# Two FFNs beside a patch search on one core: a new order of work on all five engines, transposes by DMA, moments on the vector engine

## What is computed

```python
y = einsum('ncij,vc->nvij', patches, w_mask) / (x_norm * w_norm)
idx = argmax(y.reshape(NL, -1))                       # over 512 x 9
integrate = max_act * max_sim + w_mask[max_ch] * (1 - max_sim)
h = leaky_relu(concat([integrate, sim_map_max]) @ w_i1.T + b_i1, 0.2)
vcs = tanh(h @ w_i2.T + b_i2)
h2 = relu(vcs @ w_l1.T + b_l1) @ w_l2.T + b_l2        # then out_p = einsum with w_conv
x = x + fold(out_p)
def ffn(t): return qlinear(relu(qlinear(ln(t), W1, b1)), W2, b2)   # q: x, W, b to e5m2
t = t + ffn(t)                                        # FFN 0
xn = ln_c(x); s = (xn * xn).sum(axis=1)
x = x + xn / (2 + 1e-4 * conv5x5(s)) ** 0.75
t = t + ffn(t)                                        # FFN 1
```

## Time and profile before

| | us |
|---|---|
| median of 3 runs (lowest, highest) | 3559.91 (3558.04, 3561.16) |
| the profiled execution | 3554.84 |
| its span | 3553.0 |
| busy: PE, ACT, DVE, POOL | 3011.0, 2832.7, 2778.1, 2566.0 |
| PE's granted clock, mean | 0.958 |

### The profile page before, as it was taken

The page is one execution under the profiler, slowest core; times in us unless marked ns, Lnnn a source line. Parts: engine busy times, 40 slices in busy tenths (PEclk is TensorE's granted clock), DMA queues, the critical chain, the costliest instruction groups (busy, mean ns, idle before and its releaser), DMA issues. The chain is left out here.

```text
span 3553.0 us, 62660 instructions
## 1 busy us (share of the span) xinstructions
PE 3011.0 (85%) x18190; PEld 1688.2 (48%) x18190; DVE 2778.1 (78%) x10043; ACT 2832.7 (80%) x7303; POOL 2566.0 (72%) x3993
## 2 busy tenths in 40 slices
PE   5888888888888888888888888888888888888755
PEld 2444454454545445445544545454444555445432
DVE  6777888888888888888888888888888888888631
ACT  0444788888888888888888888888878888888977
POOL 2455787777778777777877777787777778777753
PEclk9999999999999999999999999999999999999855
DMA  3111121211112121111212111121212112121000
GB/s 88 38 45 47 45 63 52 65 54 57 61 57 62 52 67 51 57 61 56 62 52 67 52 58 60 57 62 52 66 51 64 55 57 62 52 66 42 24 31 35
DMA packets 64607, 195.78 MB, mean 55 GB/s; under 512 B 11394, under 2 KB 14732, under 8 KB 64268
## 3 DMA queue, kind: packets, MB, share of 16 engines
q1 hardware_dynamic: 54028, 172.89, 15.1%
q0 software_dynamic: 10240, 18.89, 2.1%
HBM read 134.72 MB, written 57.02 MB: 54 GB/s over the span
## 5 line engine op out<-in xcount | busy, mean ns | idle before, releaser
L527 ACT ACTIVATE ffn_hid<-banks 128x384 f16<-128x384 f32 x2304 | 1026.8, 487 | 260.0 <-PE banks L370 236.7
L393 PE MATMUL banks<-wcT,xc 128*128 128x512 f32 x2304 | 1187.8, 618 | 50.2 <-DVE mx L745 43.4
L745 DVE TENSOR_REDUCE mx<-banks 128x1 f32<-128x512 f32 x1152 | 781.4, 687 | 428.8 <-PE banks L393 427.6
L370 PE MATMUL banks<-ffn_xT,w1q 128*128 128x384 bf16 x2304 | 668.8, 343 | 177.3 <-ACT ffn_hid L527 138.0
L994 POOL TENSOR_TENSOR ffn_f<-ffn_y,b2q 128x864 f16<-128x864 f16 x256 | 465.3, 1818 | 288.3 <-DVE nb L731 209.7
L370 PEld LDWEIGHTS banks<-ffn_xT,w1q 128*128 128x128 bf16 x2304 | 226.1, 98 | 775.8 <-ACT ffn_hid L527 589.4
L393 PEld LDWEIGHTS banks<-wcT,xc 128*128 128x128 f32 x2304 | 414.5, 196 | 282.8 <-issue 140.8
L825 DVE TENSOR_SCALAR ffn_hid<-ffn_hid,b1q 128x1152 f16<-128x1152 f16 x768 | 405.8, 551 | 139.0 <-ACT ffn_hid L527 138.6
L996 POOL TENSOR_TENSOR x<-x,ffn_f 128x864 f32<-128x864 f32 x256 | 466.6, 1823 | 20.1
L560 ACT ACTIVATE ffn_x<-x,cols 128x96 fp8e5<-128x96 f32 x1152 | 461.3, 456 | 0.0
L560 ACT ACTIVATE ffn_x<-x,nb,roots 128x96 fp8e5<-128x96 f32 x1152 | 425.1, 456 | 0.0
(11 more groups left out here) (153 smaller groups left out, 4178.6 us busy)
## 6 DMA issues: line engine op xcount, KB each, us to landing
xt<-x_tok_in SPq DMA_DIRECT2D x128, 432.0 KB, 3.2
xc<-x_chan_in SPq DMA_DIRECT2D x128, 432.0 KB, 3.6
out_tok<-x SPq DMA_DIRECT2D x128, 432.0 KB
win<-x_tok_in,xrow POOLq DMA_INDIRECT x128, 2.6
wrow<-vector_table,vidx POOLq DMA_INDIRECT x128, 2.9
shift<-shift_in SPq DMA_DIRECT2D x1, 960.0 KB
vector_table<-wtab SPq DMA_DIRECT2D x1, 384.0 KB, 2.9
w1raw<-w_in SPq DMA_DIRECT2D x1, 288.0 KB
```

The lines of the kernel that those rows point to most:

```text
L370: last = pe.matmul(bank[:, 0:GW], w1q[:, ffn.layer, c * P:(c + 1) * P], ffn.xT[:, g * GW:(g + 1) * GW], start=True, stop=True)
L393: last = pe.matmul(ps_score[score_bank(j)], xc[p][:, j, :], wcT[:, :], start=True, stop=True)
L527: return nc.scalar.activation(dst, src, ACT.Copy)
L745: nc.vector.tensor_reduce(mx[p][:, j:j + 1], ps_score[score_bank(j)], AX.X, ALU.max).then_inc(score_taken, 1)
```

## The change

The fp8 pixels of an FFN are written in pairs, turned by a DMA transpose that SP issues (`turn`), and read by PE in place of the three transposing units; the nine hidden units are cut 512, 512, 128 columns wide. The moments move from POOL to DVE, where they alternate with the pick; three sums of the pick become one product and one reduction. POOL's two adds of an output are taken apart (`ffn_bias`, `ffn_output`). And the order of each engine's step is new. The diff, cut:

```diff
+COLUMNS = [(0, 512), (512, 1024), (1024, J * P)]
-UNITS = G + HC * G + 2
+UNITS = HC * G + 2
...
+                self.x8 = sb(f"{name}_x8", [P, PAIRS, P, 2], F8)
+                self.xT = sb(f"{name}_xT", [P, PAIRS, P], F16)
...
+            def turn(ffn, tile):
+
+                sp.wait_ge(ffn.x8_ready, tile + 1)
+                wait_past(sp, ffn.filled, tile * UNITS - 2)
+                sp.dma_start_transpose(ffn.xT[:, :, :], ffn.x8[:].rearrange("p a c t -> p (a c t)").bitcast(F16)
+                                       ).then_inc(ffn.turned, 16)
...
+            def body(k):
+                if k.back is not None:
+                    turn(ffn0, k.back)
+                if k.pre is not None:
+                    turn(ffn1, k.pre)
+                load(Step(k.k + 1))
                 if k.rtail is not None:
                     sp.wait_ge(x4_ready, k.rtail + 1)
...
-                        for i in range(J // G):
-                            last = pe.matmul(bank[0:C, i * P:(i + 1) * P], ffn.x8[:, u * G + i, :],
-                                             ident_b[:, :], start=True, stop=True)
...
+                            pe.wait_ge(ffn.turned, (tile + 1) * 16)
+                        c0, c1 = COLUMNS[g]
+                        pairs = ffn.xT[:, c0 // (2 * P):(c1 + P) // (2 * P), :].bitcast(F8).rearrange(
+                            "p a (x t) -> p a t x", t=2)
...
+                        last = pe.matmul(bank[:, 0:c1 - c0], w1q[:, ffn.layer, c * P:(c + 1) * P], pairs,
+                                         start=True, stop=True)
...
+                wait_past(pe, inpT_ready, f2)
...
                 scores(0, 2)
-                if k.tail is not None:
-                    fill(ffn0, k.tail, G + HC * G, 2)
+                hidden_units(ffn1, k.rear, 0, 2)
+                out_units(ffn0, k.tail, k.tail_p, 0)
+                out_units(ffn0, k.tail, k.tail_p, 1)
+                hidden_units(ffn1, k.rear, 2, 2)
+                scores(2, 3)
...
+                take_hidden(ffn1, k.rear, 7, 2)
+                norm1(k, 0, XA)
+                norm1(k, XA, XA + 1)
+                take_hidden(ffn0, k.back, 0, 2)
+                norm1(k, XA + 1, XA + 2)
+                take_hidden(ffn0, k.back, 2, 2)
+                norm1(k, XA + 2, J)
+                take_hidden(ffn0, k.back, 4, 2)
+                take_out(ffn1, k.rear, k.rear_p)
+                take_hidden(ffn0, k.back, 6, 3)
...
+            def moments(tile, p):
...
+                mc.add(nc.vector.tensor_tensor(d, of(1), of(4), ALU.subtract),
+                       nc.vector.tensor_tensor(m2, of(2), of(5), ALU.add))
+                yield
+                mc.wait()
+                mc.add(nc.vector.tensor_tensor(d, d, d, ALU.mult))
+                yield
+                mc.add(nc.vector.tensor_tensor(twice[p], of(1), of(4), ALU.add))
+                yield
+                mc.wait()
+                mc.add(nc.vector.scalar_tensor_tensor(out=ssq[p], in0=d, scalar=C / 4.0, in1=m2, op0=ALU.mult,
+                                                      op1=ALU.add))
+                yield
+                mc.wait()
+                mc.add(nc.vector.scalar_tensor_tensor(out=args[:, 0:3, :], in0=ssq[p], scalar=1.0 / C,
+                                                      in1=eps[:, :, :], op0=ALU.mult, op1=ALU.add),
+                       nc.vector.tensor_copy(args[:, 3, :], ssq[p][:, 1, :]))
...
+                f1c.add(nc.vector.tensor_tensor(junk[:, :, :], pix[p][:, :, 1, :], one, ALU.mult))
+                yield
+                f1c.wait()
+                nc.vector.tensor_reduce(chosen[p][:, 0:3], junk[:, :, :], AX.X, ALU.add).then_inc(pick_ready, 1)
...
+                scores(3, WIN_TURN, factors, 2)
+                relu(ffn1, k.rear, 0)
...
+                scores(WIN_TURN, 5, factors, 2)
+                relu(ffn1, k.rear, 1)
...
+                for c in range(HC):
+                    for _ in range(2):
+                        run(moments_of, 1)
+                        run(select_of, 1)
+                    if c == HC - 1:
+                        run(moments_of)
+                        run(select_of)
+                    relu(ffn0, k.back, c)
+                round_up(ffn0, k.back)
...
+                if k.rtail is not None:
+                    ffn_bias(ffn1, k.rtail, x4_ready)
                 if k.moments is not None:
 
                     pool.wait_ge(root_ready, k.moments + 1)
                 if k.tail is not None:
+                    ffn_bias(ffn0, k.tail, x2_ready)
                     ffn_output(ffn0, k.tail, x1[k.q][:, :, :], x2[:, k.tail & RING - 1], x2_ready)
-                if k.rtail is not None:
-                    pool.wait_ge(x4_stored[k.q], landed(k.rtail, k.q))
-                    ffn_output(ffn1, k.rtail, x3[:, k.rtail3], x4[k.q][:, :, :], x4_ready)
...
-                if k.stats is not None:
-
-                    moments(k.stats, k.q)
                 if k.f1 is not None:
                     gather_pixel(k.f1, k.p)
+                if k.rtail is not None:
+                    pool.wait_ge(x4_stored[k.q], landed(k.rtail, k.q))
+                    ffn_output(ffn1, k.rtail, x3[:, k.rtail3], x4[k.q][:, :, :], x4_ready)
```

374 lines of the change are left out of this document (178 added, 196 removed).

## The result

The changed kernel takes 3903.6 us (median of 4 runs, 3887.7 to 3910.8) against 3559.0 for the one before: a ratio of 1.0966 with a 95% interval of 1.0929 to 1.1002. The forecast was 3685, the range 3390 to 3830: the sign was right, the time lies above the range and nearest to the rival called "slower by the other order at the end" (3850, chance 0.11).

A forecast was written before the change was run, and what follows sets the result against it. DVE was to become the leader: 21.8 us of work, 3.7 of stalls and 0.1 of gaps give a 25.6 us step against 24.87. Images added 118 us, ramp and drain 10: about 3685 us, range 3390 to 3830.

The forecast's parts named there:

- slower by the other order at the end: Rival: at the step's end POOL's output add beats DVE's last relu; step 27.1 us, 3850 us; chance 0.11.
- What bounds, and the mechanism: DVE becomes the leader, as POOL's adds hold its relus and roundings; step 25.6 us against 24.87.
- New places, point 2: Step's end, behind xrow: the last relu just precedes POOL's output add, and the rounding waits for that add; 1.8 us.
- Relu 0: FFN 1's first relu, behind score 3, waits out the rest of POOL's bias add; about 1.4 us a step.
- Relu 1: FFN 1's second relu meets the tail of lrn_rest on POOL; 0.2 us taken, bounds 0 to 0.85.
- The product of mlp_input: The first product of the MLP's input on DVE meets POOL's bias add for the next step; 0.3 us.
- Work of Vector: DVE gains seven moment instructions, and the pick's sums are replaced; net +1.2 us a step, to 21.8.
- What is left of the waits: With DVE as leader, only 0.1 us of gaps remain in its step.
- Transposes: PE loses 1.78 us a tile, ACT 2.70, PE's waits 1.18; DMA takes 4 us, covered; fp8 read costs 0.
- Once per image and ends: Window sums and the LRN step add 3 us per image; ramp and drain add 10 us in all.
- the late transposes' steps: Rival: DMA transposes land after more than 5 us, PE waits; steps of 25 to 28 us, about 3800; chance 0.06.
- The faster rival: Rival: DVE's stalls fall into slack, so PE's and ACT's savings show; middle 3410 us; chance 0.36.

The follow-up runs named there:

- e1: The changed kernel with FFN 1's bias add and output add moved on POOL to between the column copy and the pixel gather; 3560.7 us.
- e5: The changed kernel with only FFN 1's output add moved ahead of the pixel gather, its bias add directly behind the gather; 3754.3 us.
- run 463: Not a follow-up run: the whole profiled run of the changed kernel, in which DVE was idle 463 us; median 3903.6 us.
- e12: The changed kernel with one wait added: POOL issues FFN 1's output add only when FFN 0's rounding is over; 3620.7 us.
- e10: e8 with FFN 1's output add moved behind the gather and column copy, held until FFN 0's rounding is over; 3401.6 us.
- e8: e1 with FFN 1's relus and rounding placed later among Vector's statistics and scores, and POOL's column copy behind the pixel gather; 3460.5 us.
- e6: The kernel before, in its own order and with moments on POOL, with only the pixel transposes moved to DMA; 3698.2 us.

## Why the prediction was wrong, step by step

**What bounds, and the mechanism: right.** DVE became the leader (27.35 of the 30.1 us step), and of the 668 us by which its busy time grew, 662 are in the relus and roundings that POOL holds.

**New places, point 2: the step that failed.** "The last relu just gets in first; the output add waits 0.3 for it." The relu is due 0.5 us ahead of the output add, and still loses, for the gather holds it and the add behind the gather then goes first (e1, e5: shown). The 0.3 was no margin of starts: the sum puts the relu 1.35 us behind xrow and the gather's end 1.36 behind it, so it had a tie. In fact the relu is due 0.90 behind xrow's end, in the gather's last half microsecond. I had taken the gather as harmless without a row of the gather by xrow; in the kernel before no relu was due in it. The rows of the other gather seemed to say so: relus that became due in it, 0.2 and 0.6 us behind its start, weren't lengthened, but they were due 0.62 us or more ahead of its end. The rule that I cited, whoever issues first, tells who holds, and not who comes next when both stand waiting; behind a gather it was POOL's add, behind an add the relu. The Trainium skill ("SBUF — State Buffer", SBUF: two separate sides) warns of a Vector operation that keeps GpSimd from writing the descriptors of its DMA. This trace shows the reverse: the end of a gather's issue holds a Vector tensor_scalar (0.24 us, 125 times in e1). Had I known it, the rival with the other order would have been the likely case, not 0.11.

For the two instructions at the end of the step I had 1.8 us; they are held 1.85 + 1.33 = 3.2 a tile.

**The other holds.** Relu 0: 1.4 forecast, 0.80 measured a tile, since in 47 of 128 steps it is due at the end of the bias add and gets in ahead of the output add, and in others it comes late in that add or beside lrn_rest. Relu 1: 0.2 against 0.24. The product of mlp_input: 0.3 against 0 (L869 takes 0.154 us). The dot product beside relu 2 and FFN 1's rounding was not in my list at all: 1.16 a tile. In sum 5.0 a tile more than before, against 3.7: near the upper bound of 5.2, but by other terms, and that is luck.

**Work of Vector.** +1.2 us a step forecast, +0.04 measured (5 us in all). I priced seven moments at 0.196 each; laid between the selection's links they follow one another by some 0.11 us, and the pick's three sums went from 96.5 us to 45.8 for what stands in their place. 34 us more on the LRN's chain (L915 and L919) are in this sum too. This error hid part of the others.

**What is left of the waits.** I left 0.1 us a step; the 30.1 us step has 2.8 and the whole run 463 us. I treated Vector as a leader that PE only follows. But PE, in order, stands 5.4 us before FFN 2 with the next scores behind it, resumes at half clock, and then Vector waits for those scores (1.13 and 1.36 us in this step). e12 shows the size: 132 us less of busy time, 164 less of waiting. There is no fixed factor: the span fell by 350 us for 251 of busy time in e1, 157 for 112 in e5, 296 for 132 in e12, but only 61 for 105 in e10 against e8.

**Transposes.** Right in each term: 2.6 us to landing against 4, covered (18.6 us of PE's wait in all), the fp8 read with its step of two at no price: 691.1 us for the same 2304 x 384 columns that took 668.8, 673.0 in e1 and 664.8 in e8, where the mean clock is higher (0.931 and 0.940, here 0.896). The fit of the Trainium skill ("DMA: Bandwidth & Descriptors", Anatomy of one DMA) from which the estimate of 2.4 came is of DMAs that GpSimd issues, while SP issues these; 2.6 lies near it. But e6 shows that taking the transposes off PE and ACT gains nothing in the old order, where I had counted 3.0 us off PE's path.

**Once per image and ends.** +3 and +10 forecast. The images account for 27.6 x 13.7 = 378, the span grew by 356: the ends gave some 20 back. Small beside the rest.

**Slips in the sums.** 3683 and 5 are 3688, not 3685. By the sum's own rule stalls of 2.9 to 4.5 a step give about 3600 to 3780, not 3580 to 3790, and the late transposes' steps of 25 to 28 about 3625 to 3950, not 3570 to 3900. None of them touches the outcome.

The faster rival, at 0.36, was not reached by the change as written. e10 comes to its number, 3402 against 3410, but by another way: the holds were taken out by moving FFN 1's adds, relus and rounding and the column copy, and by one wait; they didn't fall into slack.

## What to carry to other kernels

When an engine's long operations hold another's, write down for every short operation which of them is in progress when it is due and which is queued behind it. In this case an add queued behind a gather was part of the price, and one queued behind another add was not. Put the long ones where the other engine reduces, takes statistics or reads PSUM, and if they can't be moved, one wait that starts them a microsecond later may do (e12). A hold in front of a result that an in-order engine waits for can be paid again by what stands behind it (e1, e5, e12), so ask who waits and not only how long the hold is; and test the placement, since in e10 such a hold cost less than it lasted.
